# First attention: the value projection as one block of 16 products on 128x64 tiles, where it was two passes of 16 products on 64x64 tiles

## The reference, cut to what matters

```python
q = einsum('bnd,fd->bnf', x, Wq)   # each (2, 1024, 16 * 64), then split by head
k = einsum('bnd,fd->bnf', x, Wk)
v = einsum('bnd,fd->bnf', x, Wv)
sim = einsum('bhid,bhjd->bhij', q, k) * 64 ** -0.5
sim = 50 * tanh(sim / 50)
sim = where(causal, sim, lowest)
out = einsum('bhij,bhjd->bhid', softmax(sim), v)
return einsum('bnf,df->bnd', out, Wo)
```

## Time and profile before

| what | value |
|---|---|
| runs | 1214.12, 1215.64, 1220.51 us; median 1215.64 |
| profiled execution, its own time | 1214.02 us |
| its span, first to last instruction | 1212.3 us |
| TensorE busy | 1127.0 us, 93% |
| VectorE busy | 862.3 us, 71% |
| ScalarE busy | 705.0 us, 58% |
| GpSimd busy | 522.3 us, 43% |
| mean granted TensorE clock | 0.972 of full speed |

### The profile page before, as it was taken

How to read it: one execution, slowest core, us unless ns; L and a number is a source line. 1 busy time by engine, 2 the same in 40 slices (tenths; PEclk the granted TensorE clock), 3 DMA queues, 4 the chain that set the end, 5 groups by cost and what they waited for, 6 DMA issues and landing times. The chain is left out here.

```text
span 1212.3 us, 29054 instructions
## 1 busy us (share of the span) xinstructions
PE 1127.0 (93%) x10981; PEld 628.2 (52%) x10981; DVE 862.3 (71%) x1805; ACT 705.0 (58%) x915; POOL 522.3 (43%) x529
## 2 busy tenths in 40 slices
PE   3799999999999998889997999999999999788998
PEld 1356566566665775469973222222222222547996
DVE  6466778778778465854426899999999992585442
ACT  4687877777778434512226277777777778451221
POOL 0066567667566400358843123322421331035884
PEclk9999999999999997979999999999999999797999
DMA  4001010010010102237742112221122110224665
GB/s 129 1 9 27 21 42 24 18 42 24 18 42 20 39 18 84 95 93 194 182 93 85 51 44 63 64 54 54 58 60 59 51 47 18 96 82 117 183 172 125
DMA packets 60345, 81.83 MB, mean 67 GB/s; under 512 B 23488, under 2 KB 41284, under 8 KB 59612
## 3 DMA queue, kind: packets, MB, share of 16 engines
q1 hardware_dynamic: 48180, 70.54, 19.3%
q0 software_dynamic: 10880, 8.86, 4.9%
q10 hardware_dynamic: 1192, 1.19, 0.3%
HBM read 55.12 MB, written 15.72 MB: 58 GB/s over the span
## 5 line engine op out<-in xcount | busy, mean ns | idle before, releaser
L2020 ACT ACTIVATE at_PR<-psum 128x1024 f32<-128x1024 f32 x256 | 248.1, 1021 | 107.2 <-PE psum L2267 105.2
L2089 DVE TENSOR_REDUCE at_MX<-psum 128x1 f32<-128x512 f32 x468 | 298.4, 684 | 11.7 <-PE psum L2239 8.9
L511 ACT ACTIVATE PR<-psum 128x1024 f32<-128x1024 f32 x144 | 146.3, 1021 | 72.2 <-PE psum L841 61.4
L860 PE MATMUL psum<-PR,V 64*64 64x256 f32 (+1 forms) x2560 | 172.0, 357 | 4.0 <-issue 1.5
L841 PE MATMUL psum<-Q,K 64*64 64x512 f32 (+2 forms) x1792 | 151.8, 437 | 2.1 <-ACT PR L511 2.1
L860 PEld LDWEIGHTS psum<-PR,V 64*64 64x64 f32 x2560 | 96.3, 133 | 98.9 <-issue 88.8
L516 ACT ACTIVATE PR<-PR 128x1024 f32<-128x1024 f32 x144 | 143.7, 1050 | 0.0
L2284 PE MATMUL psum<-at_PR,at_VG 128*32 128x512 f32 x1024 | 136.2, 604 | 0.8 <-POOL at_PR L1957 0.8
L1957 POOL TENSOR_TENSOR at_PR<-at_PR,at_FAC 128x512 f32<-128x512 f32 x64 | 81.1, 1267 | 101.7 <-ACT at_PR L2020 101.7
L1549 PE MATMUL psum<-moe_XGT,moe_WE 128*128 128x256 f32 x512 | 124.7, 388 | 0.2
L488 POOL TENSOR_SCALAR_AFFINE_SELECT PR<-PR 128x256 f32<-128x256 f32 (+1 forms) x80 | 54.2, 682 | 155.1 <-ACT PR L516 154.8
(11 more groups left out here) (267 smaller groups left out, 1858.9 us busy)
## 6 DMA issues: line engine op xcount, KB each, us to landing
moe_WE<-in_c_We SPq DMA_DIRECT2D x32, 768.0 KB, 4.6
XB<-at_r_dram SPq DMA_DIRECT2D x32, 256.0 KB, 3.8
at_outs_dram<-at_OTS SPq DMA_DIRECT2D x15, 256.0 KB, 2.9
moe_rows_dram<-XNS SPq DMA_DIRECT2D x2, 1152.0 KB, 12.0
moe_spare_dram<-moe_zeros SPq DMA_DIRECT2D x2, 1024.0 KB, 14.6
moe_sum_dram<-XB SPq DMA_DIRECT2D x2, 1024.0 KB, 3.8
moe_SG<-moe_spare_dram SPq DMA_DIRECT2D x8, 256.0 KB
at_KU<-in_c_max_krows SPq DMA_DIRECT2D x16, 128.0 KB
```

Source lines behind the costliest of these rows:

```text
L511: act.activation(PR[u][:, :, :], S[(b + u) % 2][:, :, :], ACT.Tanh, scale=SCALE0 / CLAMP).then_inc(z.clamped, 1)
L860: mm = pe.matmul(O[row[h], q:q + w], V[rows, b, j, row[h]], PR[u][rows, h, at:at + w], start=(first and u == 0), stop=(not first and u == ...
L2020: act.activation(PR[:, gu % PRS, 2 * r:2 * r + 2, :].rearrange("p h n -> p (h n)"), g.psum[:, 2 * r * BANK:(2 * r + 2) * BANK], ACT.Exp).t ...
L2089: dve.tensor_reduce(MX[:, c // 32 % 2, 8 * (c % 2) + 4 * pair + I % 4, khalf:khalf + 1], bank(("max", c))[:, :], AX, ALU.max).then_inc(z.r ...
```

## The change

`project` loses side 2. A new function `project_values` does the values of a step in one block: for bank x, for token tile t, for half c, one product over all 128 rows, with `start` and `stop` both set, on a tile of 128x64. That makes 16 products in all where there were two passes of 16. Each bank's `projected` increment comes after its own 8 products. The block stands in the slot k = 4, after the second half of that unit's multiply, where the second pass stood; nothing of the values is left in the slot k = 3. It waits for both key copies of the step. `part_projected` now counts two a step and not three.

```diff
                     elif first:
-                        pe.wait_ge((z.query, z.key)[side - 1], 2 * s + 2)
-                    if not first:
-                        pe.wait_ge(z.part_projected, 3 * s + side - 2)
+                        pe.wait_ge(z.query, 2 * s + 2)
+                    else:
+                        pe.wait_ge(z.part_projected, 2 * s + side - 1)
                     passed(s)
-                    for t in range(4 if side == 2 else 1):
-                        for x in range(2):
-                            rows = row[x if first else 1 - x]
-                            for c in range(2):
-                                if side < 2:
-                                    mm = pe.matmul(J[x][row[c], :], W[rows, side, row[c]], project_from(side, b, x, rows),
-                                                   start=first, stop=not first, skip_group_check=True)
-                                else:
-                                    at = b * SEQ + x * BANK + t * P + DH0 * c
-                                    mm = pe.matmul(J[x][row[c], t * P:(t + 1) * P], g.XT[rows, at:at + DH0], W[rows, 2, :],
-                                                   start=first and t == 0, stop=not first, skip_group_check=True)
-                            if not first and (side < 2 or t == 3):
-                                mm.then_inc(z.projected, 1)
+                    for x in range(2):
+                        rows = row[x if first else 1 - x]
+                        for c in range(2):
+                            mm = pe.matmul(J[x][row[c], :], W[rows, side, row[c]], project_from(side, b, x, rows),
+                                           start=first, stop=not first, skip_group_check=True)
+                        if not first:
+                            mm.then_inc(z.projected, 1)
                     if first:
                         mm.then_inc(z.part_projected, 1)
+
+                def project_values(s, b):
+
+                    pe.wait_ge(z.key, 2 * s + 2)
+                    passed(s)
+                    for x in range(2):
+                        for t in range(4):
+                            for c in range(2):
+                                at = b * SEQ + x * BANK + t * P + DH0 * c
+                                mm = pe.matmul(J[x][row[c], t * P:(t + 1) * P], g.XT[:, at:at + DH0], W[:, 2, :],
+                                               start=True, stop=True, skip_group_check=True)
+                        mm.then_inc(z.projected, 1)
...
                         k = n % NU
-                        if 1 <= k <= 4 and (n < NU or more):
-                            project(2 * p + 1 + n // NU, 1 - n // NU, (k + 1) // 2, k % 2 == 1)
+                        if 1 <= k <= 2 and (n < NU or more):
+                            project(2 * p + 1 + n // NU, 1 - n // NU, 1, k == 1)
+                        if k == 4 and (n < NU or more):
+                            project_values(2 * p + 1 + n // NU, 1 - n // NU)
```

## The result

Over 20 runs of either kernel in turn, the median went from 1217.23 to 1220.39 us, which is 3.2 us. 1220.6 was forecast, from 5.0 us on a median of 1215.64.

What follows compares the result with a forecast made beforehand. TensorE was taken as the bound; 12 blocks in the loop at 0.34 us and 3 outside at 0.31 make 5.0 us, added to the median of 1215.64 for 1220.6 us, with a range from 1216 to 1224.5.

Steps and rivals of the forecast that it cites:

- The bound: First attention, 64 to 388 us: TensorE is the bound, so what its program gains or loses moves everything behind it.
- No gap anywhere: Around the two old value passes, 0.88 us each, TensorE's neighbouring work was said to follow without idle time.
- the 1.44 us of idle: TensorE from 64 to 388 us: all its idle time in 324 us, cited against idle time swallowing the cost.
- The streaming: The new value block: 16 slots, 1.90 us with its exit, against 2 x 0.88 = 1.76 us; 0.14 us longer.
- Entering and leaving: Half multiplies around the block: the one ahead 0.14 us longer (0.11 outside the loop), the one behind 0.06 us longer.
- The sum: All 15 value blocks: 12 x 0.34 us in the loop plus 3 x 0.31 outside, 5.0 us longer.
- What was covered: Scores, key and value copies, totals and weight transfer around the block: moved starts bring no new wait.
- B: Rival: entry gap and slow first slot are the totals' own; only 0.14 us a block recurs, 2.1 us, 1217.7; chance 0.12.
- C: Rival: no change, 1215.6 us; the excess at the totals has other causes or idle time swallows it; chance 0.06.
- D: Rival: 1222.6 us; the shape change costs more between packed 64x64 work, from 0.41 us a block; chance 0.13.
- E: Rival: faster, 1208 us; the block would need at least 0.41 us less a step than 1.76 us; chance 0.02.

Runs made afterwards that it cites:

- two_blocks: The changed kernel with its block of 16 products cut in two blocks of 8, in slots 3 and 4; ratio 1.0064 to the kernel before.

## Why the prediction was right, point by point

**The number.** 1220.6 forecast and 1220.39 measured lie closer than the working deserves. Over 20 runs the kernel before has a median of 1217.23 and not 1215.64, 1.6 us higher, and the medians moved by 3.2 us and not 5.0: two misses that offset each other, which is luck. What the working can claim is the 5.0, inside 2.7 to 5.1, and its terms.

**The bound.** Right: every 0.31 us on TensorE came through a distance of 22.2 us to the end of the stage, 4.8 us in all. "No gap anywhere" held for the rows shown, but the 1.44 us of idle that it was backed with did not measure what it was taken for. The busy time hides a gap of 0.3 us in each step of the loop. Had the block stood ahead of that multiply, some of its price might have been hidden, and the prediction would have had no row for it. Here the block stood elsewhere and the gap stayed.

**The streaming.** Right: 1.90 us from the form at the head of the stage, 1.90 in the loop. Half as many instructions bought nothing.

**Entering and leaving.** 0.57, and 0.48 for a forecast 0.49. The totals, a block of another shape, were a good stand-in, as the price is nearly the same for each change of shape that was tried; the runs with 64x128 and 64x32 tiles add two more. The reason given for the time behind a block, weights not loaded ahead, also stands in the trace: the first weights of the half multiply behind it are loaded at 142.47, as it starts, and those of the one at 140.00 from 139.78 on. The block's own start at 140.57, with its first product. The rule quoted from the Trainium skill (TensorEngine Tiling (Array Packing), Tiling Modes), that changing the mode drains TensorE, agrees with this, also for changes of the columns alone. The 128 cycles, by estimate 0.053 us, that the Trainium skill (TensorE: Matmul & The Clock Gate, Step-by-step) gives for a drain are half of what the rows show on entering, 0.11 us at the least.

**The sum.** Mis-sized a little: 0.34 us a block in the loop, 0.31 to 0.32 measured. The term that was mis-sized is the entry in the loop: the 0.14 was read at the first change of a step, where 0.03 of it is paid once a step whatever the number of changes. The new block took that part over from the totals, whose entry fell from 0.57 to 0.54, so a block adds 0.11 on entering. In the two_blocks run, too, only the first of the three entries of a step is 0.57. 4.8 us of the stage for a forecast 5.0; 3.9 (2.7 to 5.1) by the runs.

**What was covered stayed covered.** The rows of ScalarE and VectorE that answer to the last ones of the earlier trace rows, and SyncE's to the earlier trace rows:

```profile
140.29 1.02 ACT L511 ACTIVATE PR<-psum 128x1024 f32<-128x1024 f32 x1 [0.35 <-PE psum L847]
...
143.98 1.28 DVE L643 COPY V<-psum 128x512 f32<-128x512 f32 x2
...
L459 SPq MOVE Wqkv<-in_c_Wqkv x6: 29/38/38, 120.1 to 345.5; - x6
```

ScalarE's wait ahead of the clamp of the last unit fell from 1.22 to 0.35 us, the 0.88 that the scores moved up, and bought nothing. The copies of the values start at 143.98, 1.5 us behind the block. The weights' transfer starts at 120.1, 0.2 us behind the block that ends at 119.87, and nobody waited for it.

**The rivals.** B (only the 0.14 recurs) fell with the entry at 0.57 and a block's 0.32 us; its 2.1 us also lie under the interval. C fell with the distance, and its causes with the runs: the waits of the totals cost nothing on 64x64 tiles. D needed 0.41 us a block, and none of the 15 comes near. E would have needed a shorter step.

## What to carry to other kernels

Where TensorE works back to back on 64x64 tiles, as here in float32, one block on another tile shape costs some 0.3 us: 0.31 to 0.35 on 128x64, 128x32 and 64x32, 0.38 on 64x128, and the same for 8 products as for 16. Other shapes, types and longer blocks were not tried. Count the changes of shape, not the instructions: products on 128x64 tiles that fill the array no better than 64x64 ones save no time by being half as many. And read the distance between starts, not the busy share: a wait of 0.3 us in each step of the loop was invisible in 99.6% busy, and covering it was worth as much as the change lost. Where a hardware loop and an unrolled copy run the same code, set their steps side by side: here that alone would have shown the 0.35 us.

## What the runs showed of the hardware that was not expected

- A change of the columns alone (64x64 to 64x128 or 64x32) costs at least as much as one of the rows: 0.54 to 0.57 us for 0.43 on entering, 0.15 (64x32) to 0.21 (64x128) in the block, 0.05 behind it.
- The first change of shape of a loop step costs 0.14 us on entering, each further one 0.11, and all of them 0.11 once the wait at the turn of the step is gone, as outside the loop, where that wait does not stand. Why is open.
- A multiply that waits for VectorE's copies starts 0.35 us behind their end in the hardware loop and 0.10 us behind it outside, in the same kernel. In the loop three instructions of TensorE's sequencer stand in between, each some 0.1 us behind the other; outside the trace shows none.
- Passes on 64x128 tiles with 128 moving columns take 1.09 us where the columns and the change of shape account for 1.02.
- A tile shape with fewer columns than the neighbours' can still be the better one: totals on 64x64 tiles need 1.72 us, those on 128x32 0.86 + 0.33.
